# GpSimd's queue takes half of the adjacency loads of the setup and of block 0

## What is computed

```python
def reference(x, adj, W, a1, a2, W1, W2, b):        # x 8192x128, adj 8192x8192, float32
    h = relu(layernorm(x))
    Wh = h @ W
    e = leaky_relu(Wh @ a1 + (Wh @ a2).T, 0.2)
    att = softmax(where(adj > 0, e, -9e15), axis=-1)
    x = x + relu(att @ Wh)
    h = relu(layernorm(x))
    node = h @ W1                                    # 16 columns
    m = einsum('nk,nkf->nf', node, einsum('nc,kcf->nkf', h, W2))
    return x + relu(adj @ m + node @ b)
```

## Time and profile before

| | us |
|---|---|
| timed runs, median of 3 | 1802.0 (1782.78, 1802.0, 1809.42) |
| profiled execution, time | 1774.92 |
| profiled execution, span | 1773.3 |
| TensorE matmul, busy | 1709.6 (96%) |
| VectorE, busy | 1316.8 (74%) |
| ScalarE, busy | 1089.1 (61%) |
| GpSimd, busy | 640.0 (36%) |

### The profile page before, as it was taken

How to read it: one execution, slowest core, us unless ns; L and a number is a source line. 1 busy time by engine, 2 the same in 40 slices (tenths; PEclk the granted TensorE clock), 3 DMA queues, 4 the chain that set the end, 5 groups by cost and what they waited for, 6 DMA issues and landing times.

```text
span 1773.3 us, 36102 instructions
## 1 busy us (share of the span) xinstructions
PE 1709.6 (96%) x11311; PEld 1471.3 (83%) x11311; DVE 1316.8 (74%) x1775; ACT 1089.1 (61%) x1889; POOL 640.0 (36%) x522
## 2 busy tenths in 40 slices
PE   7999799999999999999999999999999999999998
PEld 4889688888888888888888888888777788888886
DVE  7778688899898898988888798888665543433534
ACT  4644476766666766667566667664556555555554
POOL 0000056455554655655545555655553300000000
PEclk9999899999999999999999999999999999999999
DMA  9999999999999999999999999996624444453430
GB/s 234 283 291 332 336 350 289 280 329 309 281 328 307 299 280 297 336 283 280 281 278 289 320 291 297 317 308 254 255 102 152 149 167 190 154 200 143 166 142 24
DMA packets 316753, 452.23 MB, mean 255 GB/s; under 512 B 21072, under 2 KB 291616, under 8 KB 298912
## 3 DMA queue, kind: packets, MB, share of 16 engines
q1 hardware_dynamic: 297664, 356.58, 73.1%
q10 hardware_dynamic: 12208, 75.62, 10.6%
q0 software_dynamic: 6832, 19.41, 3.4%
HBM read 364.46 MB, written 87.07 MB: 255 GB/s over the span
## 4 chain that ended last, share of the span: by engine, by line
PE 45%; SPq 15%; DMA 10%; DVE 10%; issue 9%; POOL 7%; ACT 2%; ACTq 0%; POOLq 0%; DVEq 0%
SPq L289 14%; PE ot_ps L800 14%; PE ot_ps L857 13%; PE mt_ps L857 13%; DMA keep_d<-keep 9%; DVE p_sb L989 6%; PE hw_ps L769 5%; POOL prod L399 5%; DVE mt L913 2%; DMA adj_sb<-in_adj_dram 1%; ACT prod L582 1%; POOL msg L402 1%; SPq L303 1%; DVE keep L970 1%; POOL msg L414 1%
## 5 line engine op out<-in xcount | busy, mean ns | idle before, releaser
L800 PEld LDWEIGHTS ot_ps<-wh_mask,p_sb 128*128 128x128 f32 x8192 | 947.2, 193 | 100.1 <-issue 86.2
L800 PE MATMUL ot_ps<-wh_mask,p_sb 128*128 (+1 forms) x8192 | 960.3, 277 | 35.2 <-DVE p_sb L989 21.8
L989 DVE SCALAR_TENSOR_TENSOR p_sb<-zb,qcol,mt 128x1024 f32<-128x1024 uint8 (+1 forms) x512 | 750.9, 1484 | 24.0 <-PE ot_ps L800 10.5
L399 POOL TENSOR_TENSOR prod<-prod 128x1024 f32<-128x1024 f32 (+2 forms) x192 | 383.9, 2000 | 499.4 <-ACT prod L582 441.1
L516 ACT ACTIVATE wh_mask<-adj_sb 128x2048 uint8<-128x2048 f32 x256 | 487.7, 1940 | 88.0 <-DMA adj_sb<-in_adj_dram 86.3
L1037 DVE CAST mask<-adj_sb 128x1024 fp32r<-128x1024 uint8 x272 | 204.0, 757 | 244.8 <-PE mt_ps L857 243.1
L609 ACT ACTIVATE mask<-adj_sb 128x1024 fp32r<-128x1024 uint8 x240 | 255.3, 1065 | 173.5 <-PE ot_ps L857 173.3
L582 ACT ACTIVATE prod<-hw_ps,node 128x128 f32<-128x128 f32 x1024 | 278.8, 384 | 116.0 <-PE hw_ps L769 115.0
L857 PE MATMUL mt_ps<-mask,msgs 128*128 128x512 f32 x1024 | 282.6, 398 | 2.1 <-DVE mask L1037 1.1
L857 PE MATMUL ot_ps<-mask,msgs 128*128 128x512 f32 x1024 | 274.8, 390 | 1.0 <-DVE mask L1037 0.5
L769 PE MATMUL hw_ps<-wcat,hT 128*128 128x512 f32 x512 | 242.4, 596 | 0.0
(11 more groups left out here) (108 smaller groups left out, 550.6 us busy)
## 6 DMA issues: line engine op xcount, KB each, us to landing
adj_sb<-in_adj_dram SPq DMA_DIRECT2D x1024, 256.0 KB, 7.6
maskT_d<-mt ACTq DMA_DIRECT2D x64, 1024.0 KB, 8.3
adj_sb<-maskT_d SPq DMA_DIRECT2D x32, 2048.0 KB, 7.8
keep_d<-keep POOLq DMA_DIRECT2D x64, 128.0 KB, 6.4
p_sb<-keep_d SPq DMA_DIRECT2D x4, 2048.0 KB, 12.1
msg_d<-msg POOLq DMA_DIRECT2D x56, 128.0 KB, 6.6
msgs<-msg_d SPq DMA_DIRECT2D x7, 1024.0 KB, 8.9
wh_mask<-in_x_dram SPq DMA_DIRECT2D x8, 512.0 KB, 9.5
```

Of the source, the lines that this page charges most:

```text
L399: pool.tensor_tensor(prod[:, 0:n, :], prod[:, 0:n, :], prod[:, n:2 * n, :], ALU.add)\
L800: ins = pe.matmul(ot_ps[h][:, (t - t0) * ROW:(t - t0 + 1) * ROW], p_sb[:, r, t * P:(t + 1) * P], rows, start=begin and t == t0, stop=end a ...
L989: dve.scalar_tensor_tensor(p_sb[:, r, :], zbf[:, bass.ds((ib % 2) * BLK, BLK)], qcol[:, bass.ds(tile + b_, 1)], mtb[:, p, k // 2, :, 2 * ( ...
```

## The change

A piece's quadrants 2 and 3 are loaded by GpSimd instead of SP, for the four first pieces and for the other twelve of block 0. The quadrants 0 and 1 stay with SP. From block 1 on SP issues all four again. GpSimd's loads count on semaphores of their own, `adj_up[q]`; ACT waits for both in block 0. GpSimd begins with its first piece when `x_in[3]` has landed and with the next three when `x_in[5]` has. Its loads for the second turn stand ahead of `load_z(1)`, those for the third and fourth turn behind it.

```diff
-        def load_quadrants(eng, ib, jg, p, h, quadrants):
+        def load_quadrants(eng, ib, jg, p, h, quadrants, loaded=adj_in):
...
-                                  .rearrange("i r t n -> (i r) t n")).then_inc(adj_in[q], 16)
+                                  .rearrange("i r t n -> (i r) t n")).then_inc(loaded[q], 16)
...
             def load_adj(ib, jg, p, h):
-                load_quadrants(sp, ib, jg, p, h, (0, 2, 1, 3))
+                first = isinstance(ib, int) and ib == 0
+                load_quadrants(sp, ib, jg, p, h, (0, 1) if first else (0, 2, 1, 3))
...
+            def load_upper(jg, p, h):
+                q = 2 * p + h
+                if jg:
+                    pool.wait_ge(adj_cast[q], jg)
+                load_quadrants(pool, 0, jg, p, h, (2, 3), adj_up)
+
+            pool.wait_ge(x_in[3], 16)
+            load_upper(0, 0, 0)
+            pool.wait_ge(x_in[5], 16)
+            for q in range(1, 4):
+                load_upper(0, q // 2, q % 2)
+            for q in range(4):
+                load_upper(1, q // 2, q % 2)
             pool.wait_ge(z_stored, 16)
...
             start_block(0, False)
+            for jg in range(2, IT):
+                for q in range(4):
+                    load_upper(jg, q // 2, q % 2)
...
-            def cast(q, part, count, squared_before):
-
-                act.wait_ge(adj_in[q], 16 * 2 * A * count)
+            def cast(q, part, count, squared_before, first=True):
+
+                if first and not (isinstance(count, int) and count > IT):
+                    act.wait_ge(adj_up[q], 16 * A * count)
+                    if not isinstance(count, int):
+                        act.sem_inc(past_act, 1)
+                    act.wait_ge(adj_in[q], 16 * A * count)
+                else:
+                    act.wait_ge(adj_in[q], 16 * A * (2 * count - IT))
```

More of the change, by code:

```diff
@@ L194, in build @@
         adj_in = [sem(f"adj_in{q}") for q in range(4)]
+        adj_up = [sem(f"adj_up{q}") for q in range(4)]
         adj_cast = [sem(f"adj_cast{q}") for q in range(4)]
@@ L241, in build @@
         past_sp = sem("past_sp")
+        past_act = sem("past_act")
         block = ctx.enter_context(nc.Block())
@@ L627, in turn @@
                             copy_sums(ib)
-                        ahead = None if last else lambda: cast(2 * p, 1, i + 2, A * n + A)
+                        ahead = None if last else lambda: cast(2 * p, 1, i + 2, A * n + A, not finish)
                         if finish:
@@ L638, in turn @@
                             if not (last and p == 1):
-                                cast(3 if p == 0 else 1, 1, i + 1 + p, A * n)
+                                cast(3 if p == 0 else 1, 1, i + 1 + p, A * n, not finish)
                         if k == 1 and not last:
-                            cast(2 * p, 0, i + 2, A * n + A)
+                            cast(2 * p, 0, i + 2, A * n + A, not finish)
                         if k == 2 and not last:
-                            cast(2 * p + 1, 0, i + 2, A * n + A)
+                            cast(2 * p + 1, 0, i + 2, A * n + A, not finish)
             attention_loop(act, turn)
```

## The result

The changed kernel was timed twice, in two series ("jobs"), each with the kernel before beside it. Against the kernel before in the same job the ratio is 1.0144 (95% interval 1.008 to 1.0207), and in the repetition 1.0089 (1.003 to 1.0147). The first median was 1802.55 us beside 1796.91 for the kernel before. Times of one kernel spread over 40 us and more, so the ratios, which leave out the slow executions of both kernels (in the main those over 1.5% above the fastest), carry the result. A gain of 12 us was forecast; 16 to 26 us were lost. The profiled execution is 1798.86 us long, 24 us above the one of before.

The account below looks back on a forecast made before the run. It took SP's stream of loads to bound block 0, up to about 201 us. The 11.5 us term, taken as 12, with nothing for the others, gave 1802 - 12 = 1790 us, range 1770 to 1811.

Parts of the forecast that it names:

- What bounds the kernel: Up to about 201 us, SP's stream of loads sets the pace; a change ending with block 0 can win only there.
- the ceiling: Most the change could win: 20.3 us in block 0 plus 5.6 us of setup waits for `x`, about 26 us.
- the price of a row from GpSimd's queue: Block 0's `adj` loads: 52 ns for 1024 bytes from GpSimd against 64.5 from SP, 12.4 ns less a row.
- The term of 11.5 us: Block 0's stream: 64 loads moved to GpSimd's queue, with cheaper rows, shorten it by 11.5 us, taken as 12.
- The lower bound: Least gain from the moved loads in block 0: nothing, if a row costs the same from either queue.
- the queues disturb each other: Rival for block 0's stream, 5%: 5 ns more for each of 1024 rows, stream 5 us longer, 1807 us.
- The setup: Before block 0's matmuls: `x`'s seventh piece lands as before or earlier, or 9 us later; no term of its own.
- absorbed: Block 0: a TensorE start even at 76 us ends at 192 by its floor, so a later start costs nothing.
- SP's and GpSimd's issue time: Block 0's loads: SP's halved issuing gains nothing; GpSimd's 0.6 us a load, at most 1.1, is covered by idle time.
- The rival of slow issuing: Block 0, 10%: GpSimd makes its 64 loads too slowly, deciding from 2.2 us each; at 3.0 us +36 us, 1838.
- ACT's additional waits: Block 0's casts: the additional wait and counter cost well below 0.1 us each, beside waits of 3 to 7 us.
- The base: Block 0 before the change: the cost of a row from SP fell from 63.8 to 54 ns.

Follow-up runs that it names:

- the run with ACT's queue: Kernel before, with ScalarE's queue loading quadrants 1 and 3 in block 0's third and fourth turn, SP 0 and 2, no GpSimd loads: ratio 1.006.
- crossed ones: Changed kernel with SP loading quadrants 0 and 2, GpSimd 1 and 3, so each queue alternates between the partition halves: ratio 1.0202.
- both mends: Changed kernel with GpSimd's twelve early loads waiting for `x_in[7]`, and SP loading quadrants 0 and 2, GpSimd 1 and 3: ratio 0.9983.
- the setup shared: Changed kernel with only the four first pieces shared with GpSimd; from the second turn on SP loads all quadrants in order 0, 2, 1, 3: ratio 1.0192.

## Why the prediction was wrong, point by point

**What bounds the kernel.** Right as to the place: until block 1 begins, the stream of loads decides, and all of the change's effect lies there. The rest of the kernel moved unchanged. The 5.6 us of waiting for `x` that the ceiling counted were not to be had: with all of `x` first, ScalarE's wait for `adj` took their place.

**The failed step: the price of a row from GpSimd's queue.** I took 52 ns for 1024 bytes from the earlier trace rows, from a queue that mostly stores. As a loader of `adj` it made 62.5 ns in block 0, and 0.835 x 352 / 1223 = 240 ns for 3.25 KB, 76 ns for 1024 bytes, from 31 to 53 us. The term of 11.5 us was nothing. The lower bound, that a row costs the same from either queue, was the truth of this term. The Trainium skill, "DMA: Bandwidth & Descriptors", section "Issuing engines are not separate DMA queues", says that a second issuer saves only issue time; the run with ACT's queue agrees, 73 ns with one queue and with two. That rule would have given no change, though, and what was measured is a loss.

**What was missing: which partitions a queue writes.** The kernel before alternates, 0, 2, 1, 3; I had noted that order and given it no price. The change leaves SP with 0 and 1, one half of the partitions, and takes the alternation away as soon as GpSimd's queue is empty. Rows then cost 84 to 91 ns. SP alone, with runs of one half, paid 75 to 88 ns and 1.67% of the time. A rival of this mechanism was not among mine; "the queues disturb each other" at 5 ns a row had neither its place nor its price. The Trainium skill has a likely ground for it: "SBUF — State Buffer", section "Door 1: The DMA port swizzle (why `[64,N]` ≈ `[32,N]`)", says that partitions 0 to 63 reach only 8 of 16 ports for DMA, as do 64 to 127. That the ports are the reason is not shown by a run here. The same page, in the section "Can I just issue two DMAs to hit both halves?", gives 6% for two concurrent DMAs on the two halves. In one queue of many loads the order of the halves was worth more here in most windows: 75 to 91 ns a row against 50 to 76.

**The setup: right mechanism, wrong size, wrong conclusion.** I had written that GpSimd's larger packets might win the engines, with `x` 9 us later. It was 16.3 us later, since GpSimd's queue got 4.5 times the bytes of SP's, and beside the 16 loads that I had counted it had four of the second turn, issued at 36.50, before `x` had landed. What I did not count was that `x` goes in packets of 512 bytes, and that the queues take turns by packet (700 to 700 from 36 to 48 us). And I had called this absorbed, because the same bytes cross before block 0's last load. That fails at the buffers: there are four. When they are full, the stream stops until a cast frees one, and the casts wait for the setup. SP stood for 18.8 us where the earlier trace rows has no such wait, and some 4 us of engine time are gone. The rest of the 16 us was absorbed, as far as the estimates above go: TensorE's floor ends at 199, and the dearer rows account for what else block 1 was late. How far the delay is absorbed depends on what else holds up the stream. With one-sided queues, moving the wait to `x_in[7]` won 3 us at block 1's start; with crossed ones it took the ratio from 1.0202 to 0.9983, of which half a per cent to one is the difference between the jobs. The two causes do not add up: each alone cost about as much as both. That the later one hides part of the earlier would explain it, but is not shown.

**SP's and GpSimd's issue time.** Right: 0.583 us for a load of 256 rows, between the 0.570 of the earlier trace rows and the 0.6 that I took. The rival of slow issuing needed 2.2 us and did not occur, and no wait for VectorE showed in it (maximum 0.676). **`load_z(1)`** moved from 77.05 to 93.84, 17 us and not a few, because the setup was late; nobody waited for it. **ACT's additional waits** did not show.

**The base.** I read the fall from 64 to 54 ns within block 0 as a property of the kernel. Rows of 53 to 58 ns late in block 0 are in three of its four profiles, but the fourth has 66 to 73. (The 1957 packets of that sum are not in the earlier trace rows; the profile has 1956 from 175 to 181 us.)

The measured median of 1802.55 lies in the stated range, on the other side of the kernel before.

## What to carry to other kernels

When loads are split between queues, keep in each queue what the order before did: each queue should alternate between the partition halves, since queues do not stay in step and each will at times run alone. Queues took turns by packet here, so the one with larger packets gets more bytes, and a load in small rows that the critical path waits for should not be issued beside it. A wait on that load's semaphore ahead of the bulk took the overtaking away; it delayed the bulk (the first matmul was at 70 to 73 us, not at 67 to 69), and the time with both mends was that of the kernel before. A delay can only be absorbed by a stream that still has free buffers to fill: count them before calling it covered. And read the share of the DMA engines before calling a wait of the issuing engine lost time: 18.8 us of SP's waiting were 4 us of the stream.

## What the runs showed of the hardware that I had not expected

- GpSimd's queue and SP's take turns packet by packet: 700 to 700 from 36 to 48 us, at 3.27 KB and 0.5 KB a packet. From 31 to 53 us that made 3.97 MB to 0.89 MB. ACT's against SP's with equal packets: 0.50 to 0.44 MB.
- Rows of 1 KB from a queue left with one half of the partitions cost 82 to 91 ns, those of a queue that changes the half every four loads 75 to 88, and alternating ones 50 to 76.
- The cost of alternating rows is near 55 ns or near 70 ns for tens of microseconds at a time, and two executions of the same kernel can differ in it (with the setup shared 74 and 63 ns from 144 to 148 us, 73 and 56 from 172 to 176). No run here says why.
